# Banded attention in a four-layer kernel: far products straight from strided operands, and rows of maxima, z and statistics at other places in the step order

## The reference, cut to what matters

```python
def _L0_attn_a_ref(x, Wqkv, bqkv, Wout, bout, Wgate, bgate, pos_bias):
    OFFSETS = sorted(set(range(0, 33)) | {48, 64, 96, 128, 192, 256, 384})
    H, HD = 16, 16
    q, k, v = jnp.split(x @ Wqkv + bqkv, 3, axis=-1)      # then b h n d
    scores = jnp.stack([jnp.einsum('bhnd,bhnd->bhn', q, _shift(k, delta, n)) for delta in OFFSETS], axis=-1) * HD ** -0.5
    scores = scores + pos_bias.T[None, :, None, :]
    scores = jnp.where(invalid, -jnp.inf, scores)         # token < offset
    alpha = jax.nn.softmax(scores, axis=-1)
    out = sum(alpha[..., i:i + 1] * _shift(v, delta, n) for i, delta in enumerate(OFFSETS))
    gate = jax.nn.sigmoid(x @ Wgate + bgate)
    return flat(out) * gate @ Wout + bout
...
x = x + _L0_attn_a_ref(_layernorm(x), ...)
```

## Time and profile before

| | |
|---|---|
| median of 3 runs | 3304.84 us (3300.21 to 3306.57) |
| profiled execution | 3302.18 us, span of its instructions 3300.4 us |
| busy in the span | PE 82%, DVE 50%, ACT 44%, POOL 27% |
| band attention | from the start to about 1366 us |
| first expert layer, dense attention, second expert layer | the rest, not touched |

### The profile page before, as it was taken

One profiled execution on the slowest core, in us unless ns is written; L12 is line 12 of the kernel. 1 busy time (PEld: TensorE's weight loads), 2 busy tenths in 40 slices (PEclk: granted clock), 3 DMA queues, 4 the chain that ended last, 5 costly groups with the idle time before them and its releaser, 6 DMA issues. The chain is left out here.

```text
span 3300.4 us, 102182 instructions
## 1 busy us (share of the span) xinstructions
PE 2711.5 (82%) x46240; PEld 1581.4 (48%) x46240; DVE 1657.7 (50%) x2797; ACT 1460.1 (44%) x1537; POOL 877.2 (27%) x561
## 2 busy tenths in 40 slices
PE   2678787878787887698669989898989898997897
PEld 1455565656555655443334444444444444443443
DVE  3455444444444444520656666666666666664501
ACT  1344444444444453342225555555555554555522
POOL 3343434343435242000322222222212121211002
PEclk8789888889897988799779999999999999999998
DMA  8333323232433332459132222222212222220498
GB/s 198 81 99 75 96 68 99 66 99 72 105 79 98 75 99 50 124 241 421 61 90 59 59 59 59 59 59 56 61 41 60 50 60 55 59 50 5 173 419 327
DMA packets 232618, 343.72 MB, mean 104 GB/s; under 512 B 113396, under 2 KB 141240, under 8 KB 215800
## 3 DMA queue, kind: packets, MB, share of 16 engines
q1 hardware_dynamic: 206952, 309.35, 32.2%
q10 hardware_dynamic: 25232, 27.83, 3.7%
HBM read 266.02 MB, written 68.71 MB: 101 GB/s over the span
## 5 line engine op out<-in xcount | busy, mean ns | idle before, releaser
L1375 DVE TENSOR_REDUCE b_tops<-b_slot 128x8 f32<-128x1024 f32 x576 | 680.4, 1220 | 335.5 <-PE b_slot L1224 174.1
L1417 ACT ACTIVATE b_probs<-b_slot 128x1024 f32<-128x1024 f32 x576 | 582.6, 1023 | 525.1 <-PE b_slot L1232 369.7
L515 POOL COPY a_q_far<-a_q_near 96x1024 bf16<-96x1024 bf16 x128 | 259.2, 2054 | 293.5 <-PE a_slot L592 216.8
L1174 POOL TENSOR_SCALAR_AFFINE_SELECT b_probs<-b_probs 128x1024 f32<-128x1024 f32 x128 | 139.8, 1093 | 727.7 <-ACT b_probs L1417 727.7
L1252 PE MATMUL b_outT_ps<-b_probs,b_v 128*17 128x128 f32 (+3 forms) x4608 | 317.6, 383 | 6.2 <-ACT b_probs L1417 5.5
L1232 PE MATMUL b_slot<-b_q_stack,b_k_stack 99*128 99x512 bf16 (+3 forms) x1280 | 271.5, 318 | 43.5 <-DVE b_tops L1375 32.1
L901 ACT ACTIVATE a_k_far<-a_k_near 96x1024 bf16<-96x1024 bf16 x128 | 258.3, 2067 | 101.6 <-DMA a_k_near<-parts_near_dram 90.6
L1232 PE MATMUL b_slot<-b_k_stack,b_q_stack 96*128 96x512 bf16 (+3 forms) x1280 | 265.3, 322 | 30.5 <-DVE b_tops L1375 20.1
L864 ACT ACTIVATE a_probs<-a_probs 128x1024 f32<-128x1024 f32 x128 | 133.3, 1053 | 210.1 <-DVE a_probs L795 203.5
L795 DVE TENSOR_TENSOR a_probs<-a_slot,a_bias_k 128x1024 f32<-128x1024 f32 x128 | 154.3, 1218 | 141.9 <-PE a_slot L592 141.5
L804 DVE TENSOR_REDUCE a_tops<-a_slot 128x16 f32<-128x1024 f32 x128 | 156.2, 1222 | 105.9 <-PE a_slot L592 104.8
(11 more groups left out here) (227 smaller groups left out, 4303.3 us busy)
## 6 DMA issues: line engine op xcount, KB each, us to landing
f_w_ring<-in_L_ffn_w_dram SPq DMA_DIRECT2D x128, 1024.0 KB, 17.7
parts_near_dram<-a_parts ACTq DMA_DIRECT2D x96, 256.0 KB
parts_dram<-b_parts SPq DMA_DIRECT2D x96, 256.0 KB
a_k_near<-parts_near_dram SPq DMA_DIRECT2D x128, 128.0 KB, 2.9
b_k_stack<-parts_dram SPq DMA_DIRECT2D x64, 256.0 KB, 6.9
a_q_near<-parts_near_dram SPq DMA_DIRECT2D x64, 192.0 KB, 2.9
b_q_stack<-parts_dram SPq DMA_DIRECT2D x32, 384.0 KB, 4.4
values_dram<-a_v_stage SPq DMA_DIRECT2D x16, 544.0 KB, 4.4
```

The source lines that it names most:

```text
L515: pool.tensor_copy(q_far[far][0:QK_ROWS, h, :].rearrange("p (r a) -> p r a", r=LINKS), q_near[near][0:QK_ROWS, h, :].rearrange("p (a r) -> ...
L1174: pool.affine_select(out=blocks, in_=blocks, compare_op=ALU.is_ge, fill=0.0, base=0, pattern=[[0, NT], [1, P]], channel_multiplier=-1).the ...
L1375: ins = dve.tensor_reduce(out, src, AX.X, ALU.max)
L1417: act.activation(probs_of(b, g, u, h)[:, :], slot_of(step)[:, :], ACT.Exp).then_inc(taken_act, 1)
```

## The change

1. `turn` and the rings `q_far`, `k_far` are gone. The far products read the token-ordered stacks with a step of 16 tokens (32 bytes) in weights and moving operand. `mx` waits on PE for the DMAs of its stack, at the first head of a pair.
2. `mt` makes one copy (8 matmuls, DVE evicts it, in token order); `mrow` has four DMAs instead of eight.
3. `fp` and `mred` come after near step 3 instead of after near step 7, `mt` and `mrow` ahead of the far steps instead of after far step 3, and the fillers of place 4 after `mrow`.
4. From the third batch on, the first half of `z` for the next batch comes at the end of group 0 instead of early in group 1. The two `stats` steps of the finished batch go from the end of group 1 to place 4 of groups 1 and 2.

```diff
-            return [("ot", b - 1, 3), ("gmul", b - 1)], [], [("gate", b, 0)], [("at", b - 1, 0)], [("at", b - 1, 1)], [("gate", b, 1)]
+            return ([("ot", b - 1, 3), ("gmul", b - 1)], [], [("gate", b, 0)], [("at", b - 1, 0)], [("at", b - 1, 1)],
+                    [("gate", b, 1)] + ([("z", b + 1, 0)] if more and b >= 2 else []))
         if g == 1:
-            return ([("ot", b, 0)] + ([("z", b + 1, 0), ("zt", b + 1, 0), ("z", b + 1, 1)] if more else []), [],
-                    [("zt", b + 1, 1)] if more else [], [], [],
-                    ([("vout", b + 1, 0), ("k", b + 1, 0)] if more else []) + ([("stats", b - 1, i4) for i4 in range(2)] if earlier else []))
+            return ([("ot", b, 0)] + ([("z", b + 1, 0)] if more and b < 2 else []) + ([("zt", b + 1, 0), ("z", b + 1, 1)] if more else []), [],
+                    [("zt", b + 1, 1)] if more else [], [], [("stats", b - 1, 0)] if earlier else [],
+                    [("vout", b + 1, 0), ("k", b + 1, 0)] if more else [])
         if g == 2:
-            return [], [("ot", b, 1)], [], [], [], ([("vout", b + 1, 1)] if more else []) + [("xb", b)]
+            return ([], [("ot", b, 1)], [], [], [("stats", b - 1, 1)] if earlier else [],
+                    ([("vout", b + 1, 1)] if more else []) + [("xb", b)])
...
-            products = weave(near, early, (0, 2, 4, 6)) + place[4] + ([("fp",) + after, ("mred",) + after] if more else [])
-            products += far[0:4] + ([("mt",) + after, ("mrow",) + after] if more else []) + operands(n + 5)
+            products = weave(near, early, (0, 2, 4, 6))
+            at = products.index(near[4])
+            products[at:at] = [("fp",) + after, ("mred",) + after] if more else []
+            products += ([("mt",) + after, ("mrow",) + after] if more else []) + place[4] + far[0:4] + operands(n + 5)
             products = weave(products + weave(far[4:8], late, (0, 1, 2, 3)), through, (1, 5, 11, 17))
-            seq += ([("fparts",) + after] if more else []) + turned(n + 4) + products + [("ote", b, g)] + place[5]
+            seq += ([("fparts",) + after] if more else []) + products + [("ote", b, g)] + place[5]
...
-                            for order, rows in enumerate((q_near[ring(b, g, h // 2, BY_TOKEN)], q_far[ring(b, g, h // 2, BY_RESIDUE)])):
-                                sp.dma_start(rows[QK_ROWS:ALL_ROWS, h % 2, :], neg_rows[order][PARTS * h:PARTS * (h + 1), :]).then_inc(mrows_in[h // 2], 16)
+                            sp.dma_start(q_near[ring(b, g, h // 2, BY_TOKEN)][QK_ROWS:ALL_ROWS, h % 2, :], neg_rows[PARTS * h:PARTS * (h + 1), :]
+                                         ).then_inc(mrows_in[h // 2], 16)
...
-                        ins = pe.matmul(dst[RES * r2:RES * (r2 + 1), at:at + 64], left[1][rows, h, RES * r:RES * (r + 1)],
-                                        right[1][rows, h, RES * r:RES * (r + 1)], start=start, stop=True, skip_group_check=True)
+                        ins = pe.matmul(dst[RES * r2:RES * (r2 + 1), at:at + 64], left[rows, h, r:N:LINKS],
+                                        right[rows, h, r:N:LINKS], start=start, stop=True, skip_group_check=True)
...
-                        pe.wait_ge(turned_q, turns)
-                        pe.wait_ge(turned_k, turns)
+                        if h % 2 == 0:
+                            n = ring(b, g, h // 2, BY_TOKEN)
+                            pe.wait_ge(stacked[n], STACK * count(f"stack{n}", "stack", b, g, h // 2))
...
-                        for at, i in [(at, i) for at in (AT_ROWS, 2 * AT_ROWS) for i in range(NT)]:
-                            ins = pe.matmul(dst[at:at + HG * PARTS, i * P:(i + 1) * P], neg_parts[:, :, :, i].rearrange("p h a -> p (h a)"),
+                        for i in range(NT):
+                            ins = pe.matmul(dst[AT_ROWS:AT_ROWS + HG * PARTS, i * P:(i + 1) * P], neg_parts[:, :, :, i].rearrange("p h a -> p (h a)"),
...
-                            ins = dve.tensor_copy(neg_rows[1].rearrange("c (r a) -> c r a", r=LINKS),
-                                                  src[2 * AT_ROWS:2 * AT_ROWS + HG * PARTS, :].rearrange("c (a r) -> c r a", r=LINKS))
+                            ins = dve.tensor_copy(neg_rows, src[AT_ROWS:AT_ROWS + HG * PARTS, :])
...
-                        act.activation(neg_rows[0], slot_of(step)[AT_ROWS:AT_ROWS + HG * PARTS, :], ACT.Copy).then_inc(rows_kept, 1)
...
-                            act.activation(k_far[far][0:QK_ROWS, h, :].rearrange("p (r a) -> p r a", r=LINKS),
-                                           k_near[near][0:QK_ROWS, h, :].rearrange("p (a r) -> p r a", r=LINKS), ACT.Copy).then_inc(turned_k, 1)
```

More of the change, by code:

```diff
@@ L176, in band_schedule @@
     first = [("z", 0, 0), ("zt", 0, 0), ("z", 0, 1), ("zt", 0, 1)] + projection("q", 0, 0) + projection("k", 0, 0)
-    first += operands(0) + operands(1) + operands(2) + operands(3) + turned(0) + turned(1)
+    first += operands(0) + operands(1) + operands(2) + operands(3)
     first += [step for i4 in range(2) for step in (("v", 0, i4), ("vout", 0, i4))]
-    first += [("mx", 0, 0, h) for h in range(HG)] + turned(2) + [("fparts", 0, 0)] + projection("q", 0, 1)
+    first += [("mx", 0, 0, h) for h in range(HG)] + [("fparts", 0, 0)] + projection("q", 0, 1)
     first += [("fp", 0, 0), ("mred", 0, 0), ("mt", 0, 0), ("mrow", 0, 0)]
@@ L197, in band_schedule @@
             far = [("PV", b, g, 1, c) for c in range(NT)]
-            seq += [("vin", b, g), ("S", b, g, 0)] + place[0] + top[0] + [("S", b, g, 1)] + operands(n + 4) + turned(n + 3) + place[1] + top[1]
+            seq += [("vin", b, g), ("S", b, g, 0)] + place[0] + top[0] + [("S", b, g, 1)] + operands(n + 4) + place[1] + top[1]
             seq += [("S", b, g, 2)] + place[2] + [("S", b, g, 3)] + top[2] + place[3] + top[3]
             early, late, through = between(b, g)
-            products = weave(near, early, (0, 2, 4, 6)) + place[4] + ([("fp",) + after, ("mred",) + after] if more else [])
-            products += far[0:4] + ([("mt",) + after, ("mrow",) + after] if more else []) + operands(n + 5)
+            products = weave(near, early, (0, 2, 4, 6))
+            at = products.index(near[4])
+            products[at:at] = [("fp",) + after, ("mred",) + after] if more else []
+            products += ([("mt",) + after, ("mrow",) + after] if more else []) + place[4] + far[0:4] + operands(n + 5)
             products = weave(products + weave(far[4:8], late, (0, 1, 2, 3)), through, (1, 5, 11, 17))
-            seq += ([("fparts",) + after] if more else []) + turned(n + 4) + products + [("ote", b, g)] + place[5]
+            seq += ([("fparts",) + after] if more else []) + products + [("ote", b, g)] + place[5]
     b = B - 1
@@ L271, in band_attention @@
         o_bias = sb("o_bias", [P, D])
-        neg_rows = [row_home[at:at + HG * PARTS, :] for at in (AT_ROWS, 2 * AT_ROWS)]
+        neg_rows = row_home[AT_ROWS:AT_ROWS + HG * PARTS, :]
         ident16 = sb("ident16", [P, P], BF16)
@@ L291, in band_attention @@
         k_near = [sb(f"k_near{n}", [ALL_ROWS, 2, N], BF16) for n in range(BY_TOKEN)]
-        q_far = [sb(f"q_far{n}", [ALL_ROWS, 2, N], BF16) for n in range(BY_RESIDUE)]
-        k_far = [sb(f"k_far{n}", [ALL_ROWS, 2, N], BF16) for n in range(BY_RESIDUE)]
         v_stage = sb("v_stage", [P, 4, H, HD + 1])
@@ L376, in _ @@
                     pool.wait_ge(ident_made, 5)
-                    for stack in k_near + k_far:
+                    for stack in k_near:
                         pool.memset(stack[QK_ROWS:ALL_ROWS, :, :], 1.0)
@@ L507, in _ @@
                                            o_bias[:, :].unsqueeze(1).to_broadcast([P, NT, D]), ALU.add).then_inc(x_biased, 1)
[L508 to L516, removed]
             @block.sync
@@ L586, in products @@
                         at = 64 * i - lo
-                        pe.matmul(dst[BLK * c:BLK * (c + 1), at + first:at + last], left[0][rows, h, BLK * blk:BLK * (blk + 1)],
-                                  right[0][rows, h, first:last], start=start, stop=True, skip_group_check=True)
+                        pe.matmul(dst[BLK * c:BLK * (c + 1), at + first:at + last], left[rows, h, BLK * blk:BLK * (blk + 1)],
+                                  right[rows, h, first:last], start=start, stop=True, skip_group_check=True)
                     for r in range(LINKS):
@@ L613, in stacks @@
                 def stacks(b, g, pair):
-                    near, far = ring(b, g, pair, BY_TOKEN), ring(b, g, pair, BY_RESIDUE)
-                    return (q_near[near], q_far[far]), (k_near[near], k_far[far])
+                    n = ring(b, g, pair, BY_TOKEN)
+                    return q_near[n], k_near[n]
                 for step in seq:
@@ L864, in _ @@
                         act.activation(probs[h][:, :], probs[h][:, :], ACT.Exp).then_inc(probs_ready, 1)
-                    elif kind == "mt":
-                        _, b, g = step
-                        act.wait_ge(filled, count("filled", "mt", b, g))
```

(13 more changed lines are left out.)

18 lines of the change are left out of this document (6 added, 12 removed).

## The result

The changed kernel takes 3326.76 us (median; 3321.71 to 3331.75), the kernel before 3304.89 us beside it: a ratio of 1.0068, 95% interval 1.005 to 1.0087. The change makes the kernel slower by 0.7%.

What follows compares the result with a forecast made beforehand. PE was taken to set the pace in the band attention, with 219 us idle and a lowered clock. Gains of 153 us, less 6 (fp) and 60 (stride), made -87: 3215, settled at 3210 us; range 3140 to 3280.

Steps and rivals of the forecast that it cites:

- Strided operands: Far score products on PE: both operands step 32 bytes per column, 0.27 us more per block, 69 us less 9, so +60.
- fp: fp after four near steps instead of eight: PE waits a little for POOL's chain in groups with few projection pieces, +6 us.
- Copies: Turned copies on POOL and ACT vanish: 34 of the 46 us that PE waited for them are won.
- transposes: Half of the 512 transpose matmuls of the maxima on PE go, -15 us.
- Rows: PE's wait for row DMAs of maxima: fewer DMAs and earlier transposes win 36 us mid-band and 6 at the start, -42.
- z with statistics: z made a group earlier, one statistics block moved: PE's waits for z, late DVE additions and ACT's eviction shrink, -27 us.
- rival 4: The waits only move: DVE and unexplained waits on PE's instruction side take half the gain, about 3290 to 3305 us; chance 0.05.
- The clock: The granted clock in the band goes with PE's idle time, so with the waits gone it rises, -35 us.
- Rival 5: Slower: a pair's strided loads and streams are served one after the other, 166 ns per pair, about 3400 us; chance 0.10.
- Rival 3: A bf16 column pays as much as an f32 one, or loads bind: 139 instead of 60 us, 3290 us; chance 0.15.
- Rival 1: The stride is free because two streams do not exhaust the port: the 60 us fall away, 3150 us; chance 0.15.
- Far block, clock and the end of the band: Signs: far block 0.55 to 0.65 us at the upper level, PE clock above 0.90, band ending near 1275 us.

Runs made afterwards that it cites:

- the packed kernel: The changed kernel with far products reading 64 neighbouring tokens in weights and moving operand, so other far scores are computed: 3184.74 us, ratio 0.9665 to the kernel before.
- the runs with one half of the order each: The kernel before with only the maxima's steps moved ahead: 3290.48 us, ratio 0.9955; with only z and statistics moved: 3309.69 us, ratio 1.0021.

## Why the prediction was wrong

**The step that failed.** In "Strided operands" the forecast took the right row, then its excess over the packed shape, 1.06 ns per column, and halved that because an f32 column "passes about twice as long as a bf16 one", "so if each reading is what pays, it is half". What the far operands pay is not an addition to the column's own time but a floor under it: 1.9 ns for each 16 bytes opened, for the f32 columns of the earlier trace rows as for the bf16 ones here, and for these at both levels of the clock. A bf16 column is quicker to pass, so it has more to lose: 1.94 - 0.50 = 1.44 ns (124 and 32 ns per pair, 64 columns), not 0.53. Read as an absolute time, the same row gives 64 x 1.91 = 122 ns per pair. By the earlier trace rows alone that is 8 x 122 ns = 0.98 us per block in place of 0.37, 156 us over 256 blocks; with the 32 ns of a packed pair it is 8 x (122 - 32) = 0.72 us and 184, and the trace has +187 us of PE. Of these 133 us reach the end, by the ratios, where the forecast had 60. This term was too small by 73 us.

**The rest of the miss, 36 us, is on the side of the gain.** Without the stride the change gives 111 us, forecast were 147 (153 less 6 for fp). Point by point:

- Copies -34 and transposes -15, 49 together: 67 us were measured, with the clock's share. PE's idle time fell by 38 us and its running time by 27, of which 9 are transposes, not 15. With the copies gone, time at the lower level fell from 311 to 241 us, so a share of the clock's term is in these 67. About right.
- Rows -42 and z with statistics -27, 69 together: 33 to 44 were measured. This is the part that was too large. The waits named did go (39.2 to none, 18.1 to 5.2, and the 12.5 and 17.1 us are not in the list after). But idle time came back elsewhere: in the packed kernel it fell by some 75 us, not by the 97 that copies, rows, z and statistics, less fp, add up to, and the waits with no releaser rose from 61 to 105. That is the mechanism of rival 4, which had a chance of 0.05, at about half the size it was given. The sum took each wait's whole length as gain, though on one engine in order the wait behind it then shows; the runs with one half of the order each show that directly.
- The clock, -35: in the packed kernel it is there. PE's running time falls by 45 us, of which 9 are transposes; the rest are the same instructions, and the time at the lower level falls from 311 to 204 us. In the changed kernel there is nothing of it: idle time fell by 143 us and the clock stayed, 0.87 before and 0.86 after. That the clock follows the idle time, as read from the earlier trace rows, does not hold with strided operands.
- fp, +6: 5.5 us are in the list after. Right.

**The rivals.** Rival 5 alone had the direction: its threshold for slower, a far block beyond 0.94 us, is passed with 1.17. Its pair of 166 ns is measured as 124, and its time of 3400 as 3327. Its mechanism is refuted: loads and streams are not served one after the other, since either alone costs as much as both. Its packed pair of 46 ns is a whole block's time divided by 8; pairs within a block start 32 ns apart (the 104 us for loads take some 33). Rival 3 had the right row, but it too added an excess to the bf16 time. That its 139 us are near the 133 at the end is luck: PE became 187 us busier, and 68 us of its idle time went (149 to 81). Rival 1 would have been 3150; with everything packed it is 3185.

**What the prediction said would show it.** Copies gone, POOL 267 and ACT 283 us less busy, no row wait above 8 us, fp within 40 us: as said. Far block, clock and the end of the band: not.

## What to carry to other kernels

Price a strided operand by the 16-byte stretches it opens, as a floor and not as a surcharge on a packed instruction: here 1.9 ns each, for bf16 weights and moving operand alike, the longer of the two counting, so 64 bf16 columns at a step of 16 or 32 bytes take 121 to 124 ns where packed ones take 32, while a step of 4 bytes is almost free. That prices the instruction; what reaches the end depends on the idle time and the clock as well (at a step of 8 bytes, in a single run, almost nothing did). A copy on engines that have time to spare can be worth its 2 us if the products that read it twice would pay more. And do not add up the waits of one in-order engine: take one away, look at which one shows behind it, and price the change by PE's idle time, not by the wait's own row.

## What the runs showed of the hardware that was not expected

**The granted clock differed with the operand that was strided.** Both of these kernels, a single run of each, keep PE busy and differ by 4% in the length of a far block. Stretches of the one with a strided moving operand, then of the one with strided weights:

```profile
120.00:1290.00 1170.00, 1084.89 (x30920) 774.16 (x30920) 559.66 (x802) 270.39 (x262) 221.66 (x159) 0.93 0.34 86
```

```profile
120.00:1390.00 1270.00, 1196.87 (x30808) 882.60 (x30793) 559.95 (x802) 271.10 (x262) 222.74 (x159) 0.80 0.31 79
```

The far products are busy for 285.9 us in the first and 298.5 in the second, 13 us apart; the times are 98 us apart, and the second spends 508 us of the band at the lower level, the first 162. So strided weights with a packed moving operand cost more here through the clock than through the length of their blocks, and packing the moving operand of the change made it slower (3355 against 3327). What in such a block the clock answers to stays open: no run here separates it.

**Waits that no semaphore explains grew as the others went.** Between 120 and 1290 us those above 0.3 us are 50 in the kernel before (52 us) and 85 in the packed one (104 us), whose band ends at 1219. They end a median 1.40 us after the end of the latest packet of the instruction queue (1.27 to 1.57 for the middle eight tenths), while moments taken at random lie a median 2.4 to 2.5 us after one (0.5 to 5.6). That PE waits for its own instructions to be fetched is argued from this, not shown by a run; if so, the supply of instructions, some 100,000 in this program, is what a kernel with no other waits meets next.
